# Norms, roundings and silu products on VectorE instead of GpSimd, and TensorE turning the identity at twelve waits

## The reference

```python
# layer 0, attention: 8 heads of 64; keys are the 512 tokens and 77 context rows
xn, ln = layernorm(x_kv), layernorm(x_q)
attn = softmax((q / scale) @ k.T)                 # per head, 512 x 589
x = x + tanh(g_xattn[0]) * (attn @ v) @ Wout
# layer 0, feed-forward, quantised: w1, w2 rounded to -1, 0, 1
h = act_quant(layernorm(x)) @ w1.T                # act_quant: round(x * 127 / max|x|) per token
h = silu(depthwise_conv1d(h) + conv_b)            # three taps along the tokens
x = x + tanh(g_ffn[0]) * (act_quant(h) @ w2.T)
# layer 1, attention: 16 heads of 8 with rotary angles, 77 context keys
x = x + tanh(g_xattn[1]) * (softmax(rope(q) @ rope(k).T * scale) @ v @ Wo.T + bo)
# layer 1, feed-forward: 8 experts of width 64, the best 2 per token, and a shared one
w = softmax(layernorm(x) @ gate_w.T); keep top 2
x = x + tanh(g_ffn[1]) * (sum_e w_e * silu(x @ wg_e.T) * (x @ wu_e.T) @ wd_e.T + shared)
```

## Time and profile before

| | us |
|---|---|
| median of 3 runs | 305.68 |
| lowest and highest | 303.73 and 306.17 |
| the profiled execution's own time | 305.48 |
| its span, first to last instruction | 303.7 |
| PE, DVE, ACT, POOL busy | 267.9, 221.0, 167.9, 90.8 |
| mean granted TensorE clock | 0.949 |

### The profile page before, as it was taken

The page is one execution under the profiler, slowest core; times in us unless marked ns, Lnnn a source line. Parts: engine busy times, 40 slices in busy tenths (PEclk is TensorE's granted clock), DMA queues, the critical chain, the costliest instruction groups (busy, mean ns, idle before and its releaser), DMA issues.

```text
span 303.7 us, 5371 instructions
## 1 busy us (share of the span) xinstructions
PE 267.9 (88%) x1806; PEld 191.1 (63%) x1806; DVE 221.0 (73%) x501; ACT 167.9 (55%) x336; POOL 90.8 (30%) x116
## 2 busy tenths in 40 slices
PE   0899999999999989978999999999779568997786
PEld 0568677698777665756766687775358444654455
DVE  3698976786867689949888984588687747665671
ACT  1385557677562589756757676452564612451451
POOL 2100000010005607346010030045996780003571
PEclk9999999999999999999999999999997965579899
DMA  7930000000000000000000000000000100000001
GB/s 214 370 108 3 0 1 2 0 2 0 3 0 2 1 0 0 2 3 1 0 3 0 2 0 2 1 2 0 2 1 9 29 0 0 0 2 0 0 3 35
DMA packets 5855, 6.12 MB, mean 20 GB/s; under 512 B 555, under 2 KB 4805, under 8 KB 5829
## 3 DMA queue, kind: packets, MB, share of 16 engines
q1 hardware_dynamic: 4944, 4.66, 4.9%
q10 hardware_dynamic: 885, 1.12, 1.0%
HBM read 5.26 MB, written 0.52 MB: 19 GB/s over the span
## 4 chain that ended last, share of the span: by engine, by line
PE 62%; DVE 17%; POOL 9%; issue 6%; ACT 4%; DMA 1%; DVEq 0%; ACTq 0%; POOLq 0%
PE slot L551 18%; PE slot L615 10%; PE slot L596 5%; POOL XN L465 5%; PE slot L597 4%; PE slot L757 3%; PE slot L675 3%; PE slot L587 3%; POOL vex L462 2%; PE slot L580 2%; PE slot L574 2%; PE slot L588 2%; PE slot L667 2%; DVE nm L1012 2%; DVE aq L1071 1%
## 5 line engine op out<-in xcount | busy, mean ns | idle before, releaser
L823 ACT ACTIVATE PR<-slot,nm 128x589 f32<-128x589 f32 x64 | 47.7, 751 | 22.2 <-DVE nm L1012 22.0
L1012 DVE TENSOR_REDUCE nm<-slot 128x1 f32<-128x589 f32 x64 | 46.3, 763 | 8.4 <-PE slot L597 8.1
L551 PE MATMUL slot<-K,PR 128*128 128x128 f32 (+1 forms) x320 | 44.2, 279 | 1.7 <-ACT PR L823 1.4
L551 PEld LDWEIGHTS slot<-K,PR 128*128 128x128 f32 (+1 forms) x320 | 35.4, 142 | 14.0 <-ACT PR L823 9.7
L596 PE MATMUL slot<-KH,Q 128*128 128x296 f32 (+1 forms) x128 | 40.8, 337 | 1.3 <-ACT PT L786 0.6
L615 PE MATMUL slot<-PT,V 128*64 128x256 f32 (+1 forms) x320 | 38.1, 384 | 0.0
L597 PE MATMUL slot<-KL,Q 128*128 128x296 f32 (+1 forms) x128 | 36.1, 299 | 0.0
L462 POOL TENSOR_TENSOR vex<-vex,mhalf 128x2 f32<-128x2 f32 (+1 forms) x14 | 10.7, 762 | 83.5 <-DVE vex L961 83.4
L482 POOL COPY REC<-rec 128x256 f32<-128x256 f32 x16 | 6.5, 408 | 95.7 <-DVE rec L990 59.6
L772 ACT ACTIVATE PT<-slot 128x640 f32<-128x640 f32 x36 | 25.1, 705 | 8.9 <-PE slot L551 6.0
L615 PEld LDWEIGHTS slot<-PT,V 128*64 128x64 f32 (+1 forms) x320 | 21.5, 137 | 11.9 <-issue 2.7
(11 more groups left out here) (163 smaller groups left out, 539.0 us busy)
## 6 DMA issues: line engine op xcount, KB each, us to landing
CTT<-in_ctxT SPq DMA_DIRECT2D x1, 640.0 KB, 8.1
K<-in_const ACTq DMA_DIRECT2D x1, 589.0 KB, 8.3
WGU<-in_wgu SPq DMA_DIRECT2D x1, 580.0 KB, 8.7
X<-in_x SPq DMA_DIRECT2D x2, 256.0 KB, 3.9
WK<-in_wk SPq DMA_DIRECT2D x1, 512.0 KB, 6.2
out<-X SPq DMA_DIRECT2D x8, 64.0 KB, 1.5
L1W<-in_l1w SPq DMA_DIRECT2D x1, 384.0 KB, 8.1
WD<-in_wdT SPq DMA_DIRECT2D x1, 320.0 KB, 9.6
```

Of the source, the lines that this page charges most:

```text
L551: return pe.transpose(dst, src, ident[0:p, 0:p])
L823: act.activation(PR[:, s, :], W[:, K0:K0 + KEYS0], ACT.Exp, bias=nm0[:, s:s + 1], accum_out=sum0[:, b, p * 2 + f, t, e:e + 1]).then_inc(pr ...
L1012: dve.tensor_reduce(nm0[:, s:s + 1], W[:, K0:K0 + KEYS0], AX.X, ALU.max, negate=True).then_inc(max_ready, 1)
```

## The change

GpSimd keeps `rstd`, the copies of `w`, and the products of `a1`, `a3` and `m2`. The two normalisations behind each `rstd`, the two rounding steps of `n`, and the silu products of chunks 0 and 1 go to VectorE, where one fused instruction does what two did on GpSimd for a silu. Subtracting `MAGIC` from `f3`'s values becomes a copy stage, by ScalarE for four tiles and by VectorE for four. A new number behind a `+` in the plan makes TensorE turn the identity that many times into the bank that the item is about to use, once that bank is free and before the item's own waits: twelve places with 56 turns in all. The plan is written anew from its first word to its last, so other work moves too.

```diff
-x0:F0 x0:A1 k:F0 k:F2 x0:D2 k:A1 q:F4 k:A1 k:D1 v:F6 q:A1 k:D1 s:D2 q:F5 v:Ca q:D1 v:F2 q:A1 q:D1 u:F6 v:Ca
+x0:F0 x0:A1 k:F2+6 k:F4 x0:D2 k:A1 k:F0 k:A1 k:D1 q:F6 k:D1 k:A1 q:F7 s:D2 q:A1 v:F2 k:D1 q:A1 q:D1 v:F4
...
+f3:A1 f3:Cd f4:A1 f4:F3+4 f4:A1 f4:B f3:Cd f4:F6 f4:D2 f4:B f4:A1 f4:D2 f4:P2 f4:B f4:D2 f4:D3 f4:P2 a1:F3+7
+f4:D3 a1:A1 a1:P1 a2:F6+2 a1:F7 a2:D1 a1:A1 a1:P1 a2:F3+2 a4:F4 a2:D1 a4:F0 a4:F6 a4:D1 a4:D1 a4:A1 a4:B
...
-    return {"x0 D2": n == 0, "f2 P1": n < HC // 2, "f2 D2": n >= HC // 2, "f4 P2": n % TP == TP - 1}.get(f"{kind} {stage}", True)
+    return {"x0 D2": n == 0, "f4 P2": n % TP == TP - 1, "f4 D3": n % TP == TP - 1}.get(f"{kind} {stage}", True)
...
-            stage, bank = "F", int(stage[1:])
+            bank, turns = [int(n) for n in (stage[1:] + "+0").split("+")[:2]]
+            stage = "F"
...
+        def quantised(n):
+
+            item = KINDS["f3"][n - 1]
+            return qb_copied[COPIES[item]], copied(item, COPIES[item])
...
             def rstd(n, part, parts=1):
                 r = slice(part * QT // parts, (part + 1) * QT // parts)
                 pool.wait_ge(var_ready[n], part + 1)
-                return pool.tensor_tensor(vex[:, n, r], vex[:, n, r], mhalf[:, r], ALU.pow)
-
-            def normalise(n, src, m):
-                return pool.tensor_scalar(XN[:, m, :], src[:, m, :], mvx[:, n, m, 0:1], vex[:, n, m:m + 1],
-                                          ALU.subtract, ALU.mult)
...
+                pool.tensor_tensor(vex[:, n, r], vex[:, n, r], mhalf[:, r], ALU.pow).then_inc(rstd_ready[n], 1)
...
-                    link_all([pool.tensor_scalar(th, th, 1.0, None, ALU.add)])
-                    pool.tensor_tensor(YC[:, c, :], YC[:, c, :], th, ALU.mult).then_inc(silu_by_pool, 1)
-                elif kind == "f3":
-                    pool.wait_ge(rounded, n)
-                    if n > 2:
-                        pool.wait_ge(qbt_ready, n - 2)
-                    pool.tensor_scalar(QB[:, (n - 1) % 2, :], QM[(n - 1) % 2], MAGIC, None,
-                                       ALU.subtract).then_inc(qb_ready, 1)
...
                 for former in HAD[item]:
                     pe.wait_ge(*banks_free(former))
+                for _ in range(WARM[item]):
+                    turn(W[:, 0:P], ident)
...
+        def copy_quantised(engine, by, item):
+
+            n = upto(item)
+            engine.wait_ge(rounded, n)
+            if n > 2:
+                engine.wait_ge(qbt_ready, n - 2)
+            dst, src = QB[:, (n - 1) % 2, :], QM[(n - 1) % 2]
+            if by == "ACT":
+                engine.activation(dst, src, ACT.Copy, bias=-MAGIC).then_inc(qb_copied["ACT"], 1)
+            else:
+                engine.tensor_scalar(dst, src, MAGIC, None, ALU.subtract).then_inc(qb_copied["DVE"], 1)
...
             def third(item):
-
-                n = upto(item)
-                r = slice((n - 1) * TP, n * TP)
-                dve.wait_ge(xm_ready, n * TP)
-                link(dve.tensor_reduce(aq[:, r, 0], XN[:, r, :], AX.X, ALU.max, apply_absolute_value=True))
-                link(dve.tensor_scalar(aq[:, r, 3], aq[:, r, 0], 1e-5, 1.0 / 127, ALU.max, ALU.mult))
-                dve.reciprocal(aq[:, r, 2], aq[:, r, 3]).then_inc(quant_ready, 1)
+                kind, n = item[0], upto(item)
+                if kind == "n":
+
+                    dve.wait_ge(rstd_ready[1], n)
+                    tiles, r = range((n - 1) * TP, n * TP), slice((n - 1) * TP, n * TP)
+                    link_all([dve.tensor_scalar(XN[:, m, :], X1[:, m, :], mvx[:, 1, m, 0:1], vex[:, 1, m:m + 1],
+                                                ALU.subtract, ALU.mult) for m in tiles])
+                    link(dve.tensor_reduce(aq[:, r, 0], XN[:, r, :], AX.X, ALU.max, apply_absolute_value=True))
+                    link(dve.tensor_scalar(aq[:, r, 3], aq[:, r, 0], 1e-5, 1.0 / 127, ALU.max, ALU.mult))
+                    link(dve.reciprocal(aq[:, r, 2], aq[:, r, 3]))
+                    link_all([dve.tensor_scalar(XN[:, m, :], XN[:, m, :], aq[:, m, 2:3], MAGIC,
+                                                ALU.mult, ALU.add) for m in tiles])
+                    for m in tiles:
+                        dve.tensor_scalar(XN[:, m, :], XN[:, m, :], MAGIC, aq[:, m, 3:4],
+                                          ALU.subtract, ALU.mult).then_inc(xn_ready[1], 1)
+                elif kind == "f4":
+                    dve.wait_ge(rstd_ready[2], n // TP)
+                    for m in range(n - TP, n):
+                        normalise(2, X2, m, XN[:, m, :], xn_ready[2])
+                elif kind == "a6":
+                    dve.wait_ge(rstd_ready[3], n)
+                    for m in range(part_tiles(item).start, part_tiles(item).stop):
+                        normalise(3, X3, m, XN[:, m, :], xn_ready[3])
```

More of the change, by code:

```diff
@@ L106 @@
[L106 to L115, removed]
@@ L173, in orders @@
             mine = range(bank, bank + 1 + wide(item))
-            bank_of[item], had[item] = bank, list(dict.fromkeys(holder[i] for i in mine if i in holder))
+            bank_of[item], warm[item], had[item] = bank, turns, list(dict.fromkeys(holder[i] for i in mine if i in holder))
             holder.update({i: item for i in mine})
-    return order, bank_of, had, copier
-ORDER, BANK_OF, HAD, COPIES = orders()
+    return order, bank_of, had, copier, warm
+ORDER, BANK_OF, HAD, COPIES, WARM = orders()
 NTH = {x: n for n, x in enumerate(x for x, stage in ORDER["PE"] if stage == "F")}
@@ L516, in work, with power, halves @@
                                        ALU.mult).then_inc(upw_ready, 1)
-            def normed(item):
-                kind, n = item[0], upto(item)
-                which, part = {"n": (1, n - 1), "f4": (2, n // TP - 1), "a6": (3, n - 1)}[kind]
-                link_all([rstd(which, part, PARTS)])
-                for m in range(part * TP, part * TP + TP):
-                    normalise(which, {"n": X1, "f4": X2, "a6": X3}[kind],
-                              m).then_inc(xm_ready if kind == "n" else xn_ready[which], 1)
-            def last(item):
-                kind, n = item[0], upto(item)
-                if kind == "n":
-                    tiles = range((n - 1) * TP, n * TP)
-                    pool.wait_ge(quant_ready, n)
-                    link_all([pool.tensor_scalar(XN[:, m, :], XN[:, m, :], aq[:, m, 2:3], MAGIC,
-                                                 ALU.mult, ALU.add) for m in tiles])
-                    for m in tiles:
-                        pool.tensor_scalar(XN[:, m, :], XN[:, m, :], MAGIC, aq[:, m, 3:4],
-                                           ALU.subtract, ALU.mult).then_inc(xn_ready[1], 1)
-                else:
-                    m = n - 1
-                    pool.wait_ge(hid_ready, n)
-                    pool.wait_ge(upw_ready, n)
-                    pool.tensor_tensor(HM[:, m % QT, 0:MH], HM[:, m % QT, 0:MH], HB[:, m % 2, :],
-                                       ALU.mult).then_inc(hidw_ready, 1)
-            walk("POOL", {"P1": work, "P2": normed, "P3": last})
+            def power(item):
+                n = upto(item)
+                rstd(*{"n": (1, n - 1, PARTS), "f4": (2, n // TP - 1, PARTS), "a6": (3, n - 1, PARTS)}[item[0]])
+            def halves(item):
+                n = upto(item)
+                pool.wait_ge(hid_ready, n)
+                pool.wait_ge(upw_ready, n)
+                hm = HM[:, (n - 1) % QT, 0:MH]
+                pool.tensor_tensor(hm, hm, HB[:, (n - 1) % 2, :], ALU.mult).then_inc(hidw_ready, 1)
+            walk("POOL", {"P1": work, "P2": power, "P3": halves})
         @block.tensor
@@ L921, in second @@
                     if n % QT == 1:
-                        for c in range(HC):
-                            act.wait_ge(*silu(("f2", item[1], c)))
+                        act.wait_ge(silu_ready, HC * (n // QT + 1))
                     if n > 2:
```

117 lines of the change are left out of this document (54 added, 63 removed).

## The result

The changed kernel takes **293.87 us** (median of 4 runs, 292.03 to 295.5) against 305.75 before (4 runs). The ratio is 0.9637, with a 95% interval of 0.9572 to 0.9702: 3.6% less. The forecast was 296.1. The profiled execution took 293.82 us, its span is 291.8, its mean granted clock 0.976 (0.949 before).

What follows compares the result with a forecast made beforehand. The prediction took TensorE's work as the bound up to 207 us, then a tail chain of waiting steps. 303.7 - 13.7 + 4.0 + 0.3 = 294.3, and 1.8 from span to execution, gave 296.1 us; range 289.5 to 304.

Steps and rivals of the forecast that it cites:

- The tail's chain: Dependent steps of the second sequence after the last `w`: predicted to shrink from 96.8 to 83.1 us, 13.7 less.
- from `f3` to `a2`: Tail stage, 19.1 us before: faster norm, cheaper `QB` and a full clock in `a2` were to give 16.4.
- I let the two cancel: Before the last `w`: VectorE's added work against GpSimd's removed latencies, net zero, 3 us to the good side, 6 bad.
- The sign that was named for this case: Wrong on the good side if TensorE's idle time before the last `w` falls from 8 to under 5 us.
- VectorE's queue: Rival before the last `w`: VectorE, with 237 us of work, becomes the bound; 313.6 us, or 306 at full clock; chance 0.08.
- `n`: 10.9 predicted: First tail stage, last `w` to `f2`, 15.2 us before: 4.3 less from norms, roundings, earlier `a6` and fewer waits.
- `f2`: 10.9 predicted: Tail stage, 12.4 us before: VectorE becomes the bound with taps and four silus, a gain of 1.5.
- `a4` and `a6`: Tail stage, 29.1 us before: full clock gives 5.1 over five items, one more `m2` front costs 0.9; 24.3.
- The last norm: Tail stage, 4.9 us before: 0.9 gained, but VectorE has eight router instructions (1.85 us) ahead; 5.0.
- The first rival: Clock stays low from `a2` to `a6` because turns do not hold it: 7.5 us more, 303.6 us; chance 0.16.
- The third rival: Tail shortens, but new waits, VectorE behind the router and turns on the path, eat half: 302 us; chance 0.14.

## Why the prediction was right, and where its steps were off

**The sign and the total were right, the total in part by luck.** The tail's chain is shorter by 8.0 us, not by 13.7, and the part before it gave what is missing. The mechanism of the tail holds in `n`, `f2`, and from `f3` to `a2` (16.6 for 16.4). That the last is so close is luck too: the full clock in `a2`, 1.13 us instead of 2.04, came in this execution, while in three others of the same program up to there it fell before, and the stage took 17.2 to 18.6. Three slips in the working change little: the 0.2 us between profile and median is named but not added (296.3), 16 late turns at 0.27 are 4.3 us and not 3.8, and norm, scale and rounding of two tiles take 2.5 us in one piece (209.14 to 211.63), not 3.4.

**"I let the two cancel" is the step that failed**, in the part before the last `w`. The added queue on VectorE and the removed latencies of GpSimd did not cancel: the last `w` came at 203.0 and not at 211.2. The prediction gave 3 us to the good side; it was 8. TensorE's idle time to the last `w` fell by 4.6 us (16.7, which is 206.87 - 190.21, to 12.0), and its busy time rose by 0.7 where moved products and turns should have added 4 to 5.5. The rest is in the same instructions counted shorter: the 320 turns of attention weights take 43.1 us and not 44.2, the 128 products of `KH` 40.1 and not 40.8, and so on, which I read as waits inside pipelined matmuls that the profile counts as busy. The work left on GpSimd with the new order gives 210.2, close to the 211 that was forecast, so the moved work is worth about 7 there, in one profile of each. The sign that was named for this case (idle time under 5) came: 4.5.

**VectorE's queue** did not become the bound. It got 230.0 us, not 237: two norms in a row take 0.60, and two silus 1.28, less than twice one. Between 91 and 207 it was busy for 101.6 us where I had 105. On the old plan a queue on VectorE does cost time, but in the tail and not where the rival had it: `n` becomes longer, 18.1 us, and the last `w` ends 1.1 us later than before.

**`n`: 10.9 predicted, 11.8 measured.** The router's instructions ahead of the norm were sized at 0.4 us and take 1.0 (208.16 to 209.14 in VectorE's timeline: six instructions of the program, for which the trace has eight, not four). **`f2`: 10.9 predicted, 9.6 measured.** I counted four silus ahead of `f3`; its first turn starts at 224.41, before the last one ends at 224.96.

**`a4` and `a6` were mis-sized, 24.3 predicted, 28.2 measured.** The term supposed the full clock throughout. It fell at two waits for the exponential (2.54 and 1.90 us), where no turns stood. With turns there the stage takes 24.8, in two profiles: the mechanism was right, and the clock was what the term had wrong. Such a wait does not bring a fall each time. In the profile with `QB` on GpSimd TensorE is idle from 242 to 244 and the clock stays at 1.00 up to 260; there the stage takes 26.5.

**The last norm: 5.0 predicted, 6.5 measured.** I named the queue behind the router, but took no stall: the norm then meets GpSimd's product, and takes 2.05 us for 0.60. Moved ahead of the router it is 5.1. Left on GpSimd it is 4.9, as before.

**The rivals.** The first rival, the low clock, came in part: the changed kernel's clock fell twice in `a4`. It put 7.5 us on the tail, 90.6 in all; the kernel without turns has 92.7, against 88.8 with them. So the turns keep part of that rival away, 6.2 us by the medians. The Trainium skill's page TensorE: Matmul & The Clock Gate says in Part 4: PE-mode transpose that transposes do not count as busy to the clock. By that rule kernels with and without turns would show the same clock; here the mean is 0.965 to 0.982 with them and 0.938 to 0.948 without, over four runs each. The runs do not show whether a turn, which the trace lists as MATMUL, is the transpose that the page means. The third rival (half of the gain eaten, 302) was not what happened; work or turns alone, and both on the old plan, end close to it, at 303.0 to 304.2.

**What stays open.** The new order without the rest was not run. Why TensorE's same products count shorter before the last `w`, some 4 us of the 8, is a reading. What decides whether the clock falls in `f4` in one execution and not in the next is not known. Whether the silus' 3.5 us are more than a clock that fell for longer is not shown. The last `w` ends 1.7 us later with turns on the old plan than without, with only six turns ahead of it, and the cause was not looked for.

## What to carry to other kernels

A wait disappears only when all of its parts do: an engine change and fillers that give 0.3 and 0.5% alone, and 0.6 to 1.4% in pairs with each other or with a new order, give 3.6% all together. So try them together and then take single parts out, rather than add them one by one. When an engine is relieved, look at what queues up behind what on it (a root, two norms, then the one value that TensorE wants), not at its busy share. Fill TensorE's longest waits of a chain too: here the clock fell, in most profiles, at the ones that were left. And profile more than one execution before a stage's length is put down to an edit: the same program gave 16.6 to 18.6 us for one stage.

## What the hardware showed beyond that

- A VectorE `tensor_scalar` pair of 128x128 takes 0.60 us alone and 2.05 or 2.29 us while GpSimd multiplies 128x512 tiles. GPSIMD Engine Reference of the Trainium skill says in section 1. Specifications that the SBUF interfaces are shared with VectorE; the traces agree, and the price of these two meetings is 1.4 and 1.7 us.
- Turns of an identity, which nobody reads, raised TensorE's mean clock: it was between 0.938 and 0.948 in four runs without them, and between 0.965 and 0.982 in four runs with 56 of them. At one place they are not sure to hold it: with the same turns the clock was 1.00 up to 243 us in one profile and fell at 231 to 234 in three.
- The changed kernel's time follows the mean clock of the run: 292.03 us at 0.982, 293.82 at 0.976, 295.5 at 0.965. Of the unprofiled runs only the mean is known, so where a fall lands in them stays open, and differences of 1 to 2 us between such kernels need more runs than there were.
